# Cross-attention and coupled feed-forward: part of a first layer moved into attention slots, and the front of the feed-forward stage written in half dozens of products

## The chip, the cores and the metric

The kernel runs on one core of a Trainium2 chip. The metric is the device time of one execution in microseconds (us). Before the change it is 1096.31 us, the median of 3 runs (1096.15 to 1098.32).

## The reference

`x` is 64 batches of 256 tokens with 256 features, the context 64 batches of 120 keys with 256 features. All is float32.

```
n    = layernorm(x)
# attention, 16 heads of 16 features
s    = exp(log_C) * tanh(scale * (q_h . k_h) / 4)         # masked keys: -inf
x    = x + concat_h(softmax(s) @ v_h) @ W_out.T
# feed-forward: 3 cycles on u = layernorm(x)
gf   = sigmoid(gelu(gelu(mean_tokens(u) W1g + b) W2g + b) W3g + b)   # one number per batch
repeat 3 times:
    tf = sigmoid(gelu(gelu(gelu(u W1 + b1) W2 + b2) W3 + b3) W4 + b4)  # one number per token
    c  = 0.1 + range * (0.7 gf + 0.3 tf - 0.5) * 2
    u  = u + c * twist(u)            # twist permutes and negates quarters of the features
x    = x + u
```

The first layer is linear before its gelu, so the kernel holds `u W1` (in the tile `f_t`, "straight") and `twist(u) W1` (in `v_t`, "twisted") and updates these two with `c` instead of multiplying by W1 again in cycles 2 and 3.

## The kernel before, in words

**Stages.** The 64 batches are taken in 8 groups of 8. `slots()` yields one attention slot per batch, in software pipeline: in slot i TensorE makes the scores of batch i, the weighted values of batch i-1, the output projection of i-2, and transposes the normalised features of batch i-3 (`LAG` = 3). After the slot in which the last batch of a group has passed that transpose, `slots()` yields a feed-forward stage for the group. In the text, slot k (0 to 7) of a group is the slot with (i-3) mod 8 = k, so slot 7 is the last before the stage. Slots 0 to 7 of group 1 begin on TensorE at about 174, 182, 190, 199, 207, 215, 224 and 232 us of the span; its stage begins at 241 us.

**A slot.** Each engine has its own instruction stream, in an order that is written by hand; an instruction that waits for a semaphore holds all behind it on its engine.
- TensorE (from L1318): `scores(i,0)`, `weighted_values(i-1,0)`, `queries(i+1)`, `scores(i,1)`, `project(i-2,0)`, `keys(i+1)`, `weighted_values(i-1,1)`, `project(i-2,1)`, `norm_to_features(i-3)`. Both score products write PSUM banks 0 to 3, so `scores(i,1)` waits for the tanh of `scores(i,0)`. The weighted values write banks 4 and 5 (`PV_BANKS`), queries, keys and features bank 6, the projection bank 7.
- ScalarE (from L978): `tanh(i,0)`, `exp(i-1,1)`, `tanh(i,1)`, `exp(i,0)` (L880, L886; each 120x2048), `features(i-3)` (L896) from PSUM into `f_t`.
- VectorE (from L803): `attn_out(i-1,0)` (L678), `queries_out`, `stats` of a batch ahead, `combine` of a batch of the group before (L781, L782), `high_half`, `keys_out`, `attn_out(i-1,1)`, `divide`, `attn_features`, `residual`, `stats_2(i-2)` (L710, L716).
- GpSimd (from L552): `norm_2_scale` (needs `stats_2`), `query_scale` (needs `stats`), `norm_2` (L456, the input of `norm_to_features`), `twisted_part` (L511) and `x_part` (L520) of the group before, `query_hat` (L435, the input of `queries`), `low_half` (L529).

**The two halves.** The first layer's products run in float16, on a high and a low half of `f_t` and of the weights: three of the four combinations, two blocks of rows each, so 6 products of 128x128 by 128x512 for one half m of the output features. A group's features are taken in 4 chunks of 2 batches. `high_half` (VectorE, L725) rounds a chunk to float16, `low_half` (GpSimd, L529, once for each block k of rows) writes the rest. In the slots the chunks 0 and 1 are split: `HIGH_AT` = (2, 4) and `LOW_AT` = (3, 4, 5, 6) are the slots k of it. Chunks 2 and 3 are split in the stage: on GpSimd, the stage begins with `query_scale` and `query_hat` for two batches ahead, then `low_half` of chunk 2, the same for one more batch, then `low_half` of chunk 3.

**The stage.** Passes p = 0 to 11 are the 4 chunks in 3 cycles. TensorE runs `layer1_twisted` (L1179, banks 2 and 3), `layer1_straight` (L1192, banks 0 and 1), `layer2` (L1205), `layer3` (L1214), `layer4` (L1235, or L1232 from pass 3 on) and the global net; ScalarE the gelus (`gelu1` L912, `gelu2` L942, `gelu3` L954), `tanh4` (L966) and the copies out of PSUM (`twisted_out` L924, `straight_out` L934); VectorE `couple` (L734) and the updates of `f_t` and `v_t` (L747 to L772), which start with the tanh of pass 0. The stage's front is passes 0 to 3, in which the first layer is multiplied; there TensorE's order is

```
twisted(0) straight(0) global(0) | twisted(1) global(1) layer2(0) global(2) straight(1) layer3(0)
| twisted(2) layer4(0) layer2(1) straight(2) layer3(1) | twisted(3) layer4(1) layer2(2) straight(3) layer3(2)
| layer4(2) layer2(3) layer2(4) layer3(3)
```

with 12 products (both m) in each twisted and each straight.

Of the kernel before, what the change touches and what calls it, by code (L numbers as in the profile page):

```python
# [28 lines left out]
ALU = mybir.AluOpType  # L29
# [6 lines left out]
P = 128  # L36
# [8 lines left out]
def xattn_ffn_kernel(nc, x, ctx, mask, W_out, scale, log_C,  # L45
# [6 lines left out]
    EK = E // P  # L52
# [23 lines left out]
    with ExitStack() as stack:  # L76
# [108 lines left out]
        PV_BANKS = (4, 5)  # L185
# [44 lines left out]
        s_l1 = sem("s_l1")  # L230
        s_fhi, s_flo = sem("s_fhi"), sem("s_flo")
        s_uv = sem("s_uv")
        s_h1 = sem("s_h1")
# [17 lines left out]
        LOW_AT = (3, 4, 5, 6)  # L251
# [67 lines left out]
        def groups_before(i):  # L319

            return (i - LAG) // GROUP

# [261 lines left out]
        def _(eng):  # L584
# [88 lines left out]
            def attn_out(b, n):  # L673

                eng.wait_ge(s_pv, 2 * b + n + 1)
                if b >= 2:
                    eng.wait_ge(s_on, b - 1)
                eng.transpose(o_t[:, b % 2, 2 * n:2 * n + 2].rearrange("p c q r -> p (c q r)"),  # L678
                              banks(PV_BANKS[n])).then_inc(s_ot, 1)

# [38 lines left out]
            def high_half(g, chunk):  # L719
# [3 lines left out]
                if number >= 2:  # L723
                    eng.wait_ge(s_l1, 2 * EK * (number - 1))
                eng.tensor_copy(f_hl[:, number % 2, 0], f_t[:, :, chunk * CT:(chunk + 1) * CT]).then_inc(s_fhi, 1)  # L725

# [10 lines left out]
            def update_both(g, p):  # L737
# [5 lines left out]
                eng.wait_ge(s_uv, 2 * EK * (number + 1))  # L743
# [128 lines left out]
        def _(eng):  # L872
# [26 lines left out]
            def gelu1(g, p):  # L899
# [3 lines left out]
                for m in range(EK):  # L903
                    if cyc == 0:
                        eng.wait_ge(s_w, n_weights)
                        eng.wait_ge(s_vec0, N_SPLIT)
                        eng.wait_ge(s_l1, 2 * EK * (CHUNKS * g + chunk) + EK + m + 1)
# [7 lines left out]
            def twisted_out(g, chunk):  # L915

                number = CHUNKS * g + chunk
# [4 lines left out]
                for m in range(EK):  # L922
                    eng.wait_ge(s_l1, 2 * EK * number + m + 1)
                    eng.activation(v_t[:, m, tok], banks(V_BANKS[m]), ACT.Identity, scale=uv_scale[:, 0:1]) \  # L924
                       .then_inc(s_uv, 1)

            def straight_out(g, chunk):

                number = CHUNKS * g + chunk
                tok = slice(chunk * CT, (chunk + 1) * CT)  # L930
                eng.wait_ge(s_flo, EK * (number + 1))
                for m in range(EK):
                    eng.wait_ge(s_l1, 2 * EK * number + EK + m + 1)
                    eng.activation(f_t[:, m, tok], banks(U_BANKS[m]), ACT.Identity, scale=uv_scale[:, 0:1]) \  # L934
                       .then_inc(s_uv, 1)
# [40 lines left out]
            for kind, i in slots():  # L976
# [15 lines left out]
                else:  # L992
                    early = i * GROUP + GROUP + LAG
                    glob = banks(TR_BANK)[:, SMALL_AT:SMALL_AT + 3 * GROUP]
                    twisted_out(i, 0)
                    gelu1(i, 0)
                    straight_out(i, 0)
# [367 lines left out]
```

## Time and profile before

| what | us |
|---|---|
| median of 3 runs | 1096.31 |
| lowest, highest | 1096.15, 1098.32 |
| the profiled execution's own time | 1098.4 |
| its span, first to last instruction | 1096.6 |
| ScalarE busy in the span | 920.6 (84%) |
| TensorE busy (matmuls) | 979.9 (89%) |
| VectorE busy | 808.9 (74%) |
| GpSimd busy | 554.1 (51%) |

Times in the profile are microseconds from the start of the span. PE is TensorE, ACT ScalarE, DVE VectorE, POOL GpSimd. A timeline row reads: start, length, engine, line, operation, written tile<-read tiles, shapes, number of instructions merged into the row, and in brackets how long the engine had been idle and what released it. Matmuls overlap one another, so the next row often starts before the length of the last is over: the step from start to start is what a batch of matmuls costs.

### The profile page before, as it was taken

Reading aid. Unit: us, or ns where it says so; the run is one execution under the profiler, and the core shown is the slowest. Engines: PE = TensorE matmul, PEld = TensorE weight load, DVE = VectorE, ACT = ScalarE, POOL = GpSimd, SP = SyncE. Lnnn points to the kernel's source line nnn. Section 1 sums busy time; section 2 is a strip of 40 time slices with the busy share of each in tenths; the row PEclk is TensorE's granted clock in tenths of the full one; section 3 lists DMA queues with packets and bytes.
Section 4 is the critical chain, followed back from the end, with each engine's and each line's share of the span. In section 5 each row is a group of like instructions: output and inputs, shape, how many; then the busy total and the mean of one; then the engine's idle time right before and its main releaser. Section 6 shows DMA issues by size and latency. Waiting matters only on the chain.

```text
span 1096.6 us, 21849 instructions
## 1 busy us (share of the span) xinstructions
PE 979.9 (89%) x7260; PEld 530.3 (48%) x7260; DVE 808.9 (74%) x1738; ACT 920.6 (84%) x1153; POOL 554.1 (51%) x1053
## 2 busy tenths in 40 slices
PE   6899989899998999999999998989999899896993
PEld 4455435554355544554345543555435554453431
DVE  3888596985868666885869849698487867687285
ACT  3899778997799977998789977899779997795675
POOL 3367504884068810897028950488406881078104
PEclk7899999999999999999999999999999999998997
DMA  5433001430034200441005310143003420021002
GB/s 119 82 58 61 1 2 39 105 86 0 2 72 100 58 1 2 96 92 41 2 1 121 90 19 2 40 104 86 0 2 73 99 58 1 1 53 40 0 1 78
DMA packets 191119, 51.71 MB, mean 47 GB/s; under 512 B 165920, under 2 KB 174624, under 8 KB 191008
## 3 DMA queue, kind: packets, MB, share of 16 engines
q1 hardware_dynamic: 191008, 50.31, 21.6%
q8 instruction: 60, 0.98, 0.4%
q14 instruction: 51, 0.42, 0.1%
HBM read 33.37 MB, written 16.78 MB: 46 GB/s over the span
## 4 chain that ended last, share of the span: by engine, by line
ACT 41%; PE 30%; issue 13%; DVE 10%; SPq 2%; POOL 2%; DMA 1%; DVEq 0%; ACTq 0%; POOLq 0%
ACT probs L880 18%; ACT probs L886 14%; PE ps L1205 7%; PE ps L1192 6%; PE ps L1179 5%; ACT f_t L896 4%; PE ps L1116 3%; PE ps L1235 2%; DVE move_u L747 2%; DVE move_v L749 2%; PE ps L1214 2%; ACT h L912 2%; DVE f_t L753 2%; DVE coup L734 2%; PE ps L1147 1%
## 5 line engine op out<-in xcount | busy, mean ns | idle before, releaser
L880 ACT ACTIVATE probs<-ps,u_scale 120x2048 f32<-120x2048 f32 x128 | 257.6, 2012 | 21.4 <-PE ps L1116 21.4
L886 ACT ACTIVATE probs<-probs,exp_bias,clip 120x2048 f32<-120x2048 f32 x128 | 275.0, 2149 | 0.1
L1205 PE MATMUL ps<-h,w 128*128 128x512 f32 x384 | 184.4, 606 | 12.9 <-ACT h L912 12.1
L1116 PE MATMUL ps<-q_t,k_t 32*120 32x256 f32 x2048 | 150.0, 407 | 34.6 <-ACT probs L880 33.1
L475 POOL TENSOR_TENSOR c<-tok_c 128x16 f32<-128x16 f32 x8 | 1.8, 224 | 329.3 <-issue 329.3
L1147 PE MATMUL ps<-wo_t,of_t 128*128 128x256 f32 x512 | 144.5, 405 | 1.8 <-DVE xy L703 1.8
L678 DVE STREAM_TRANSPOSE o_t<-ps 128x512 f32<-128x512 f32 x128 | 90.8, 709 | 74.5 <-PE ps L1132 74.2
L1132 PE MATMUL ps<-probs,va 120*32 120x256 f32 x2048 | 138.4, 388 | 2.0 <-ACT probs L886 2.0
L1116 PEld LDWEIGHTS ps<-q_t,k_t 32*120 32x120 f32 x2048 | 95.1, 181 | 65.0 <-issue 60.5
L1147 PEld LDWEIGHTS ps<-wo_t,of_t 128*128 128x128 f32 x512 | 87.3, 190 | 51.0 <-issue 42.1
L1205 PEld LDWEIGHTS ps<-h,w 128*128 128x128 f32 x384 | 66.8, 188 | 87.7 <-issue 64.4
L942 ACT ACTIVATE h<-ps,b 128x512 f32<-128x512 f32 x96 | 65.6, 684 | 39.1 <-PE ps L1205 39.1
L912 ACT ACTIVATE h<-f_t,b 128x512 f32<-128x512 f32 x128 | 85.1, 715 | 11.6 <-DVE f_t L772 8.2
L1179 PE MATMUL ps<-f_hl,w1t_hl 128*128 128x512 f16 x384 | 90.1, 385 | 0.0
L734 DVE TENSOR_SCALAR coup<-coup,c_tok,c_batch 128x256 f32<-128x256 f32 x128 | 49.3, 427 | 54.7 <-ACT coup L966 53.6
L1192 PE MATMUL ps<-f_hl,w_hl 128*128 128x512 f16 x384 | 88.2, 379 | 0.0
L529 POOL TENSOR_TENSOR f_hl<-f_t,f_hl 128x512 f16<-128x512 f32 x64 | 75.2, 1186 | 19.9 <-DVE f_hl L725 19.9
L1132 PEld LDWEIGHTS ps<-probs,va 120*32 120x32 f32 x2048 | 53.8, 110 | 57.5 <-issue 19.5
L435 POOL TENSOR_SCALAR q_hat<-xy,neg,rstd 128x256 f32<-128x256 f32 x128 | 77.4, 613 | 4.2 <-POOL rstd L425 3.8
L456 POOL TENSOR_SCALAR f_hat<-xy,neg,rstd 128x256 f32<-128x256 f32 x128 | 74.4, 587 | 5.4 <-POOL rstd L446 5.4
L725 DVE CAST f_hl<-f_t 128x1024 f16<-128x1024 f32 x32 | 23.6, 738 | 70.0 <-PE ps L1192 70.0
L912 ACT ACTIVATE h<-ps,b,uv_scale 128x512 f32<-128x512 f32 x64 | 48.9, 776 | 31.2 <-PE ps L1192 31.1
(128 smaller groups left out, 1826.5 us busy)
## 6 DMA issues: line engine op xcount, KB each, us to landing
xy<-in_x_dram SPq DMA_DIRECT2D x64, 256.0 KB, 3.3
out_dram<-xy SPq DMA_DIRECT2D x64, 256.0 KB, 2.0
cbuf<-in_ctx_dram SPq DMA_DIRECT2D x64, 120.0 KB, 2.8
va<-in_ctx_dram SPq DMA_DIRECT2D x64, 120.0 KB, 3.6
tok_c<-coup SPq DMA_DIRECT2D x256, 0.5 KB, 2.0
move_v<-in_L_xattn_W_out_dram SPq DMA_DIRECT2D x1, 256.0 KB, 5.6
move_u<-in_L_ffn_cn_w_dram SPq DMA_DIRECT2D x1, 256.0 KB, 3.4
w<-in_L_ffn_cn_w_dram SPq DMA_DIRECT2D x1, 128.0 KB, 3.1
```

The lines of the kernel that those rows point to most:

```text
L435: eng.tensor_scalar(q_hat[:, at, t, :], xy[:, b % XR, t * E:(t + 1) * E], neg1[:, at, t:t + 1], rstd1[:, at, t:t + 1], ALU.add, ALU.mult). ...
L529: eng.tensor_tensor(f_hl[:, slot, 1, k], f_t[:, k, tok], f_hl[:, slot, 0, k], ALU.subtract) \
L678: eng.transpose(o_t[:, b % 2, 2 * n:2 * n + 2].rearrange("p c q r -> p (c q r)"), banks(PV_BANKS[n])).then_inc(s_ot, 1)
L880: eng.activation(probs[:, b % 2, n * HALF:(n + 1) * HALF, :].rearrange("k h q -> k (h q)"), banks(SCORE_BANK, 4)[0:KEYS, :], ACT.Tanh, sca ...
L886: eng.activation(p, p, ACT.Exp, scale=clip[0:KEYS, 0:1], bias=exp_bias[:, b:b + 1]).then_inc(s_exp, 1)
L912: eng.activation(h1[:, p % 2, m, :], source, ACT.Gelu, bias=b1[:, m:m + 1], scale=by) \
L1116: last = eng.matmul(banks(SCORE_BANK + r)[0:KEYS, odd * S:(odd + 1) * S], k_t[rows, b % 2, odd, n, :], q_t[rows, b % 2, n, :], start=True, ...
L1132: last = eng.matmul(banks(PV_BANKS[n])[j * SLOT:(j + 1) * SLOT, (c % 2) * S:(c % 2 + 1) * S], va[:, b % VR, h, :], probs[:, b % 2, h, :], ...
L1147: last = eng.matmul(banks(X_BANK)[:, t * E:(t + 1) * E], of_t[:, k, t * P:(t + 1) * P], wo_t[:, k, :], start=(k == 0), stop=(k == EK - 1))
L1179: last = eng.matmul(banks(V_BANKS[m]), w1t_hl[:, w, k, m * P:(m + 1) * P], halves[:, f, k, :], start=(n == 0), stop=(n == len(PRODUCTS) - 1))
L1192: last = eng.matmul(banks(U_BANKS[m]), w1_hl[:, w, k, m * P:(m + 1) * P], halves[:, f, k, :], start=(n == 0), stop=(n == len(PRODUCTS) - 1))
L1205: last = eng.matmul(banks(bank), w2[:, k, :], h1[:, p % 2, k, :], start=(k == 0), stop=(k == EK - 1))
```

## The change

For each group, the first layer of chunk 0 (four half dozens: twisted m = 0, 1, straight m = 0, 1) is computed in the slots 4 to 7, one half dozen a slot, into bank 5, and VectorE brings it to `v_t` or `f_t`. The weighted values use bank 4 alone. The stage then has only chunks 1 to 3 to multiply, and its order on TensorE and ScalarE is written out by half dozens. `low_half` is done in slots 2, 3, 5, 6.

```
-        PV_BANKS = (4, 5)
+        PV_BANK = 4
+        SIDE_BANK = 5
-        LOW_AT = (3, 4, 5, 6)
+        LOW_AT = (2, 3, 5, 6)
+        SIDE_AT = (4, 5, 6, 7)
+        SIDES = 2 * EK
...
             def high_half(g, chunk):                                    # VectorE
-                if number >= 2:
-                    eng.wait_ge(s_l1, 2 * EK * (number - 1))
+                if chunk == 2:
+                    eng.wait_ge(s_sl1, SIDES * (g + 1))
+                elif number >= 2:
+                    eng.wait_ge(s_ul1, EK * (...))
...
+            def side_out(g, part):                                      # VectorE
+                kind, m = part // EK, part % EK
+                eng.wait_ge(s_sl1, SIDES * g + part + 1)
...
+                dst = (v_t, f_t)[kind]
+                eng.tensor_scalar(dst[:, m, 0:CT], banks(SIDE_BANK), uv_scale[:, 0:1], None, ALU.mult).then_inc(s_side, 1)
...
                     if 0 <= nxt < NB:
                         keys_out(nxt)
+                    if side_of(i) is not None:
+                        side_out((i - LAG) // GROUP, side_of(i))
                     if 0 <= here < NB:
                         attn_out(here, 1)
...
             def weighted_values(b, n):                                  # TensorE
-                if after_ffn(b + 1):
-                    eng.wait_ge(s_h2, PASSES * groups_before(b + 1) - 1 + n)
-                elif b:
-                    eng.wait_ge(s_ot, 2 * (b - 1) + n + 1)
+                if after_ffn(b + 1) and n == 0:
+                    eng.wait_ge(s_h2, PASSES * groups_before(b + 1) - 1)
+                if 2 * b + n:
+                    eng.wait_ge(s_ot, 2 * b + n)
...
+            def layer1_side(g, part):                                   # TensorE
+                kind, m = part // EK, part % EK
+                halves = f_hl[:, CHUNKS * g % 2]
+                weights = (w1t_hl, w1_hl)[kind]
+                if part == 0:
+                    eng.wait_ge(s_vec0, N_SPLIT)
+                    eng.wait_ge(s_flo, EK * (CHUNKS * g + 1))
+                if part == 0 and g:
+                    eng.wait_ge(s_h2, PASSES * g)
+                elif part:
+                    eng.wait_ge(s_side, SIDES * g + part)
+                for n, (w, f, k) in enumerate(PRODUCTS):
+                    last = eng.matmul(banks(SIDE_BANK), weights[:, w, k, m * P:(m + 1) * P], halves[:, f, k, :],
+                                      start=(n == 0), stop=(n == len(PRODUCTS) - 1))
+                last.then_inc(s_sl1, 1)
...
                         if 0 <= nxt < NB:
                             queries(nxt)
+                        if side_of(i) is not None:
+                            layer1_side((i - LAG) // GROUP, side_of(i))
                         if 0 <= i < NB:
                             scores(i, 1)
```

`gelu1` of pass 0 now reads `f_t` (scale 1.0) after `s_side`, and `twisted_out`, `straight_out`, `layer1_twisted` and `layer1_straight` take one m at a time. The new front of the stage, with a half dozen written as t(chunk,m) or s(chunk,m), is

```
TensorE: global(0) t(1,0) t(1,1) s(1,0) s(1,1) global(1) layer2(0) global(2) t(2,0) layer3(0) t(2,1) layer4(0)
         layer2(1) s(2,0) layer3(1) s(2,1) layer4(1) t(3,0) layer2(2) t(3,1) layer3(2) s(3,0) layer4(2) s(3,1)
         layer2(3) layer2(4) layer3(3)
ScalarE: gelu1(0) global gelu, t_out(1,0) t_out(1,1) gelu1(1) global gelu, gelu2(0) global tanh, gelu3(0)
         s_out(1,0) s_out(1,1) tanh4(0) t_out(2,0) t_out(2,1) gelu2(1) gelu1(2,m0) gelu3(1) gelu1(2,m1) tanh4(1)
         s_out(2,0) s_out(2,1) t_out(3,0) gelu2(2) gelu3(2) t_out(3,1) gelu1(3,m0) tanh4(2) s_out(3,0) gelu1(3,m1)
         gelu1(4) gelu2(3) s_out(3,1) gelu3(3) gelu2(4) gelu1(5)
```

From pass 5 on nothing is changed.

## Rows read from the trace of the kernel before

**Rows 1.** The profile page: the chain that ended last, by engine.

```profile
ACT 41%; PE 30%; issue 13%; DVE 10%; SPq 2%; POOL 2%; DMA 1%; DVEq 0%; ACTq 0%; POOLq 0%
```

**Rows 2.** Busy time by stage: window, length, then each engine's busy us.

```profile
215.22:223.63 8.41, 7.56 (x83) 4.84 (x82) 7.47 (x19) 8.41 (x9) 6.57 (x13) 1.00 0.27 79
240.65:272.70 32.05, 30.98 (x138) 14.29 (x135) 18.26 (x41) 24.08 (x41) 14.93 (x25) 1.00 0.09 16
```

**Rows 3.** Timeline of ScalarE, slots 4 and 7 of group 1.

```profile
212.06 2.02 ACT L880 ACTIVATE probs<-ps,u_scale 120x2048 f32<-120x2048 f32 x1
...
237.31 2.00 ACT L880 ACTIVATE probs<-ps,u_scale 120x2048 f32<-120x2048 f32 x1
...
241.86 2.15 ACT L886 ACTIVATE probs<-probs,exp_bias,clip 120x2048 f32<-120x2048 f32 x1
```

**Rows 4.** Timeline of TensorE, slots 4 and 5 of group 1.

```profile
210.39 1.14 PE L1116 MATMUL ps<-q_t,k_t 32*120 32x256 f32 x16 [0.85 <-ACT probs L880]
...
215.22 1.14 PE L1116 MATMUL ps<-q_t,k_t 32*120 32x256 f32 x16
...
217.30 0.66 PE L1091 MATMUL ps<-ident,q_hat 128*128 128x128 f32 x4
218.80 1.14 PE L1116 MATMUL ps<-q_t,k_t 32*120 32x256 f32 x16 [0.85 <-ACT probs L880]
```

**Rows 5.** Timeline of GpSimd, slots 3 to 7 and stage of group 1.

```profile
203.53 0.32 POOL L422 TENSOR_SCALAR var<-mv 128x2 f32<-128x2 f32 x1 [0.59 <-DVE mv L658]
...
209.58 1.15 POOL L529 TENSOR_TENSOR f_hl<-f_t,f_hl 128x512 f16<-128x512 f32 x1
...
218.26 0.24 POOL L443 TENSOR_SCALAR var<-mv 128x2 f32<-128x2 f32 x1 [0.85 <-DVE mv L716]
...
225.31 1.09 POOL L435 TENSOR_SCALAR q_hat<-xy,neg,rstd 128x256 f32<-128x256 f32 x2
...
240.08 1.63 POOL L435 TENSOR_SCALAR q_hat<-xy,neg,rstd 128x256 f32<-128x256 f32 x2
...
250.00 2.27 POOL L529 TENSOR_TENSOR f_hl<-f_t,f_hl 128x512 f16<-128x512 f32 x2
```

**Rows 6.** Timeline of VectorE, slot 4 of group 1.

```profile
210.42 0.65 DVE L664 COPY q_t<-ps 128x512 f32<-128x512 f32 x1
...
213.87 0.72 DVE L678 STREAM_TRANSPOSE o_t<-ps 128x512 f32<-128x512 f32 x1 [0.37 <-PE ps L1132]
```

**Rows 7.** Timeline of TensorE, stage of group 1.

```profile
240.65 2.75 PE L1179 MATMUL ps<-f_hl,w1t_hl 128*128 128x512 f16 x12
...
254.43 0.65 PE L1214 MATMUL ps<-h,w 128*64 128x256 f32 x4
255.01 2.76 PE L1179 MATMUL ps<-f_hl,w1t_hl 128*128 128x512 f16 x12
257.62 1.03 PE L1235 MATMUL ps<-h,w4rep 128*128 128x256 f32 x4
```

**Rows 8.** Timeline of VectorE, stage of group 1: the couplings of passes 0 to 3.

```profile
259.40 1.12 DVE L734 TENSOR_SCALAR coup<-coup,c_tok,c_batch 128x256 f32<-128x256 f32 x2 [3.88 <-ACT coup L966]
...
267.85 0.73 DVE L734 TENSOR_SCALAR coup<-coup,c_tok,c_batch 128x256 f32<-128x256 f32 x2 [2.00 <-ACT coup L966]
...
274.61 0.73 DVE L734 TENSOR_SCALAR coup<-coup,c_tok,c_batch 128x256 f32<-128x256 f32 x2 [0.69 <-ACT coup L966]
...
280.80 0.73 DVE L734 TENSOR_SCALAR coup<-coup,c_tok,c_batch 128x256 f32<-128x256 f32 x2
```

**Rows 9.** Timelines of group 0: GpSimd in slot 3, TensorE in slot 4.

```profile
76.44 1.62 POOL L529 TENSOR_TENSOR f_hl<-f_t,f_hl 128x512 f16<-128x512 f32 x1
...
78.56 0.66 PE L1091 MATMUL ps<-ident,q_hat 128*128 128x128 f32 x4
```

**Rows 10.** Timeline of TensorE, stage of group 7, the last.

```profile
1015.18 4.62 PE L1179 MATMUL ps<-f_hl,w1t_hl 128*128 128x512 f16 x12
...
1033.64 1.03 PE L1235 MATMUL ps<-h,w4rep 128*128 128x256 f32 x4
```

More of the change, by code:

```diff
@@ L321, in groups_before, with uv_done, side_of @@
             return (i - LAG) // GROUP
+        def uv_done(g, chunk):
+            return 2 * EK * ((CHUNKS - 1) * g + chunk)
+        def side_of(i):
+            at = (i - LAG) % GROUP
+            return SIDE_AT.index(at) if i >= LAG and at in SIDE_AT else None
         def paired(p):
@@ L897, in features, with gelu1 @@
                                    ACT.Identity, scale=F_SCALE, accum_out=f_sum[:, k, at:at + 1]).then_inc(s_ft, 1)
-            def gelu1(g, p):
+            def gelu1(g, p, halves=range(EK)):
                 (cyc, chunk), n = slot_of(p), PASSES * g + p
@@ L902, in gelu1 @@
                     eng.wait_ge(s_l2, n - 1)
-                for m in range(EK):
-                    if cyc == 0:
+                for m in halves:
+                    if cyc == 0 and chunk == 0:
                         eng.wait_ge(s_w, n_weights)
-                        eng.wait_ge(s_vec0, N_SPLIT)
-                        eng.wait_ge(s_l1, 2 * EK * (CHUNKS * g + chunk) + EK + m + 1)
+                        eng.wait_ge(s_side, SIDES * (g + 1))
+                        source, by = f_t[:, m, 0:CT], 1.0
+                    elif cyc == 0:
+                        eng.wait_ge(s_ul1, EK * ((CHUNKS - 1) * g + chunk - 1) + m + 1)
                         source, by = banks(U_BANKS[m]), uv_scale[:, 0:1]
@@ L1169, in layer1_twisted @@
+            def layer1_twisted(g, chunk, m):
                 number = CHUNKS * g + chunk
                 halves = f_hl[:, number % 2]
-                eng.wait_ge(s_vec0, N_SPLIT)
                 eng.wait_ge(s_flo, EK * (number + 1))
-                for m in range(EK):
-                    if chunk == 0:
-                        eng.wait_ge(s_tanh, 2 * min(GROUP * g + GROUP + LAG, NB))
-                    else:
-                        eng.wait_ge(s_uv, 2 * EK * (number - 1) + m + 1)
-                    for n, (w, f, k) in enumerate(PRODUCTS):
-                        last = eng.matmul(banks(V_BANKS[m]), w1t_hl[:, w, k, m * P:(m + 1) * P], halves[:, f, k, :],
-                                          start=(n == 0), stop=(n == len(PRODUCTS) - 1))
-                    last.then_inc(s_l1, 1)
@@ L1183, in layer1_straight @@
-            def layer1_straight(g, chunk):
+                if chunk == 1:
+                    eng.wait_ge(s_tanh, 2 * min(GROUP * g + GROUP + LAG, NB))
+                else:
+                    eng.wait_ge(s_uv, uv_done(g, chunk - 2) + m + 1)
+                for n, (w, f, k) in enumerate(PRODUCTS):
+                    last = eng.matmul(banks(V_BANKS[m]), w1t_hl[:, w, k, m * P:(m + 1) * P], halves[:, f, k, :],
+                                      start=(n == 0), stop=(n == len(PRODUCTS) - 1))
@@ L1227, in layer4 @@
                 if paired(p):
[L1228 removed]
+                    eng.wait_ge(s_uv, uv_done(g, CHUNKS - 1))
                 for b in range(CB):
```

166 lines of the change are left out of this document (95 added, 71 removed).

## The prediction, made blind

> **What bounds the kernel now.** I read the chain that ended last first, then busy time by stage, then the timelines of one group, engine by engine. The chain [rows 1] is ScalarE's for 41% and TensorE's for 30%: no single engine holds the whole span. The stages tell why [rows 2]. An attention slot takes 8.41 us and ScalarE is busy for all 8.41 of them; TensorE is busy 7.56 of them. The front of the feed-forward stage takes 32.05 us and TensorE is busy 30.98 of them. So moving products from the front into the slots takes work from the stage where TensorE is full and gives it to one where it has some room. In a slot that room is 0.85 us, one gap, in which TensorE has finished the queries and waits for the tanh to free the score banks [rows 4].
>
> All below is worked out for group 1 on its own time axis; groups 2 to 6 repeat it. I call a time "shifted" when it is given less the delay that the slots have built up.
>
> **Slots, middle groups: what is added.** One half dozen on TensorE, at half of the 2.60 us from one dozen to what follows it (255.01 to 257.62) [rows 7]: 1.30 us. One evacuation on VectorE, PSUM to SBUF, 128x512: the copy of the same size takes 0.65 [rows 6]. `low_half` moves from slot 4 to slot 2 on GpSimd, 1.15. No DMA is moved or added; the weighted values lose a bank, but each waits only for the transpose of the product before, which VectorE starts right behind it (213.87, 0.72 long [rows 6]) and TensorE comes back 2.5 us later, so I cost that at nothing. If that transpose came late, it would hold TensorE; the side evacuation stands ahead of it on VectorE and delays it by some 0.15.
>
> *Step 1, the first half dozen waits.* It needs both low halves of chunk 0. The second is made in slot 3, last on GpSimd, before and after the change: 209.58 plus 1.15 [rows 5]. The low half added in slot 2 pushes it: 1.15, of which the 0.59 that GpSimd waited in slot 3 [rows 5] takes half. It ends at 211.28. TensorE has its queries done at 209.7 and would be ready, so the half dozen runs from 211.35 to 212.65 and `scores(i,1)` starts at 212.65 in place of 210.39 [rows 4]. Its tanh starts 1.18 later, at 213.83, in place of 212.06 [rows 3]: ScalarE loses 1.77 in slot 4.
>
> *Step 2, three slots at TensorE's pace.* Between `scores(i,1)` at 210.39 and the next slot at 215.22 TensorE has 4.83 of work without a gap [rows 4]; from there to the end of the queries 2.68 (217.30 less 215.22 plus 0.60); the half dozen 1.30. That is 8.81 a slot, over the 8.41 of ScalarE. Three of them bring `scores(i,1)` of slot 7 to 212.65 + 26.43 = 239.08.
>
> *Step 3, the queries come late.* `q_hat` on GpSimd hangs on `stats_2` and `stats`, which VectorE now ends later: its attention work in slot 4 begins at 216.3 instead of 213.87 [rows 6], as the weighted values do. GpSimd's slot 5 starts 2.4 later than at 218.26 [rows 5], `q_hat` ends at 228.8 instead of 226.4 [rows 5], TensorE wants it at 228.35. It waits 0.5 there and 0.2 in slot 7. Together 239.78; the tanh of slot 7 starts at 240.96 instead of 237.31 [rows 3]. **The slots cost 3.65 us a group.**
>
> **The stage, middle groups: what is taken away.** 24 products, 5.2 us of TensorE, and 4 copies of ScalarE. Shifted times from here, the last exponential at 241.86 [rows 3]. The stage now begins with the global net, which needs ScalarE's last features, so TensorE starts at 242.05, not 240.65 [rows 7]. The four half dozens of chunk 1 run until 247.6, then `layer2(0)` and the small nets until 250.1. (`gelu1(0)`, behind the exponential and its table load, ends at 246.5, in time.)
>
> *Step 4, a second wait for GpSimd.* t(2,0) needs the low halves of chunk 2, which end at 250.00 + 2.27 = 252.27 [rows 5]. Before, TensorE came for them at 255.01 [rows 7] and they cost nothing; now it comes at 250.1. GpSimd stands behind `stats` of VectorE, whose slot 7 ends 0.43 later (shifted). So t(2,0) starts at 252.75 and 2.6 us of the 5.2 are given back. `layer3(0)`, which needs nothing of this, is queued behind it.
>
> *Step 5, to the couplings.* t(2,0) 1.30, `layer3(0)` 0.58 (254.43 to 255.01 [rows 7]), t(2,1) 1.30: `layer4(0)` at 255.93 against 257.62 [rows 7]. The coupling of pass 0 starts at 257.7 against 259.40 [rows 8]. VectorE needs 6.07 us a pass (267.85 to 274.61, less 0.69) and waited 2.00 and 0.69 before passes 1 and 2 [rows 8]. With TensorE without a gap from 252.75 on, `layer4(1)` is at 262.5, `layer4(2)` at 269.6, so pass 1 does not wait (264.1) and pass 2 hardly (270.5). Pass 3 has its tanh at 277.3, behind `gelu1(4)` and `gelu1(5)` on ScalarE, and its coupling at 278.0 against 280.80 [rows 8]. From there VectorE is without a gap in both. **The stage gives 2.8 less 0.05, 2.75 us.**
>
> Net of a middle group: 3.65 - 2.75 = +0.9, six times: +5.4.
>
> **Group 0.** No group before it, so GpSimd is idle when its low halves come: the one of slot 3 ends at 78.06, TensorE's queries at 79.2 [rows 9]. Step 1 falls away. TensorE's excess of 0.4 a slot for four slots, less the lead that the scores had, is 1.2; the stage gives 2.4. Net -1.2.
>
> **Group 7.** From its slot 5 on there are no new scores: the half dozens run in empty time, and no batch ahead keeps GpSimd from chunk 2. The stage starts slow (12 products in 4.62 us [rows 10] against 2.75 [rows 7]); with that, 24 products, `layer2(0)`, t(2,0), `layer3(0)` and t(2,1) put `layer4(0)` at 1029.0 against 1033.64 [rows 10]. Another 1.1 comes from the waits of VectorE as in step 5. Net -5.7.
>
> **Sum:** 5.4 - 1.2 - 5.7 = -1.5 us. The profiled execution has a span of 1096.6 and a time of 1098.4; the sum gives 1095.1 and 1096.9. The median before is 1096.31, 2.1 under the profiled one; against it 1094.8, and I say 1095.
>
> **Bounds of what the trace does not show.** The side evacuation: nothing if it falls in VectorE's wait (0.37 before the transpose [rows 6]), 0.65 in each of four slots if VectorE's round were the bound; I take 0.15, since VectorE is busy 7.47 of 8.41. The switch between float16 and float32 products: within the 1.30, or 0.1 more each way by the dozen's own length of 2.75 against 2.60 [rows 7]. The stage's written-out order: at worst only the 1.7 of pass 0 is kept (a loss of 1.05 a group), at best pass 3's coupling comes as early as VectorE can, 276.6 (a gain of 1.4). For six groups that is from -8 to +6.
>
> **A row and a rule.** The same two-instruction `q_hat` took 1.09 in slot 5 and 1.63 in slot 7 [rows 5], so something of VectorE holds GpSimd now and then for some 0.5. The Trainium skill (SBUF - State Buffer, Who interferes with whom) says that VectorE and GpSimd share a port pair as a lock, that the loser waits for the whole instruction, and that a VectorE instruction with one input from PSUM outside the 2-port modes does not take it. By that rule the side evacuation adds nothing to GpSimd, as in my sum, but VectorE's two-input instructions, which move against GpSimd's, may; no row here shows the new alignment.
>
> **Rivals.**
> A. *The first wait does not bite* (step 1): chunk 0's low halves are there in time. Then `scores(i,1)` of slot 4 starts at 210.8, the slots cost 1.8, a middle group nets -0.95: -5.7 - 6.9 = -12.6, 1084. Against it: the row at 209.58 stands in every group from 1 on.
> B. *Neither wait bites*: the whole 5.2 of TensorE pays, the stage gives 5.4 and the slots cost 1.2; -4.2 in seven groups and -5.7: -35, 1061. Against it stand the two rows of L529 [rows 5]. For it, only that GpSimd is idle much of the span.
> C. *Slower: GpSimd becomes the bound of slots 4 to 7.* Its chain of scale, features, twisted, x and query parts is held by VectorE once more in each of the slots 3, 5 and 6, 0.43 to 0.54 each (1.63 less 1.09 [rows 5]). All three lie on TensorE's path to the first half dozen or to the queries: +1.3 a middle group, +7.8, so 1103. It decides from the point where the hold is more than 0.3 a group, as then the six groups eat what groups 0 and 7 give.
>
> **Chances.** My forecast 0.45, A 0.20, B 0.07, C 0.28. 0.2% of this kernel is 2.2 us, about what a measurement can tell from no change. My own case lies 1.5 under and moves by 6 either way: of its 0.45, 0.18 is faster, 0.15 the same, 0.12 slower. A and B are faster; C is slower but for 0.02. So faster 0.45, same 0.17, slower 0.38. My case's own range is 1087 to 1101; the range takes in A and C with their spread, 1082 to 1107, and leaves B out.
>
> **What would show it.** In the profile after: GpSimd's `low_half` in slot 3 ends at 211.3 on group 1's axis and TensorE's first half dozen starts right behind it, released by it; the tanh of `scores(i,1)` in slot 4 shows an idle of 1.8; slots 5 to 7 take 8.8 to 9.3; at the stage's front TensorE idles 2 to 3 us ahead of t(2,0), released by L529, and VectorE's wait before pass 1's coupling is gone. In group 7 neither wait is seen, and its stage's couplings start 4.6 earlier after the last features. I am wrong if a middle group gets more than 2 us shorter, or if the idle time sits with VectorE's evacuation or the single bank of the weighted values.

## The result, and the profile after

The kernel after the change takes **1117.68 us** (median of 4 runs, 1116.52 to 1119.74) against 1096.63 us for the kernel before: ratio 1.019, 95% interval 1.0172 to 1.0207. It is slower, by 21 us; the forecast was 1095.0 and the range ended at 1107. The profiled execution took 1119.74 us with a span of 1118.0, which is 21.3 over the profiled execution before (1098.4); its eight groups, cut as in the table below, add up to 21.5 more.

To read where it went I cut each group at four points of the timelines: the start of ScalarE's last `tok_th` of the group before, the end of the group's last exponential, VectorE's coupling of pass 0, its coupling of pass 3, and the group's own `tok_th`.

| us | slots | last exponential to coupling 0 | coupling 0 to 3 | coupling 3 to `tok_th` | group |
|---|---|---|---|---|---|
| before, group 1 | 66.29 | 15.39 | 21.39 | 26.91 | 129.99 |
| after, group 1 | 70.28 | 15.78 | 20.83 | 26.91 | 133.81 |
| after, group 2 | 70.29 | 17.08 | 20.83 | 26.91 | 135.11 |
| before, group 0 | 113.68 | 15.39 | 21.39 | 27.26 | 177.72 |
| after, group 0 | 114.75 | 15.92 | 20.83 | 26.90 | 178.40 |
| before, group 7 | 41.06 | 35.58 | 21.39 | 25.00 | 123.04 |
| after, group 7 | 41.06 | 32.25 | 20.83 | 24.99 | 119.14 |

Groups 3, 4 and 6 are as group 1 (133.8 to 134.1), group 5 as group 2 (135.08). A middle group got 3.2 to 5.1 longer where +0.9 was forecast, group 0 0.7 longer where -1.2 was, and group 7 3.9 shorter where -5.7 was. The slots were forecast nearly right (3.65); the second column was not (-1.7 forecast, +0.4 to +1.7 measured). Group 1 of the kernel after starts 0.69 later on the axis than before, so a time of its slots compares with one of before less 0.69; in its stage, 4.67 are to be taken off (the last exponential ends at 248.68 against 244.01 [rows 3]).

The page, first the engines, then the chain that ended last by engine (it answers to [rows 1]), then three of the costliest groups (busy time, mean ns | idle time before them):

```profile
PE 994.2 (89%) x7260; PEld 529.0 (47%) x7260; DVE 829.7 (74%) x1770; ACT 905.6 (81%) x1121; POOL 554.5 (50%) x1053
...
PE 46%; DVE 15%; POOL 14%; issue 11%; ACT 11%; SPq 2%; DMA 0%; DVEq 0%; POOLq 0%; ACTq 0%
...
L912 ACT ACTIVATE probs<-ps,u_scale 120x2048 f32<-120x2048 f32 x128 | 252.9, 1976 | 39.8 <-PE ps L1156 39.0
...
L1234 PE MATMUL ps<-f_hl,w1t_hl 128*128 128x512 f16 x288 | 80.6, 427 | 20.5 <-POOL f_hl L543 20.5
```

GpSimd went from 2% to 14% of the chain though its busy time did not change; ScalarE from 41% to 11%. Both waits for GpSimd stand in the groups: the tanh now waits 39.0 us for scores (21.4 before), and `layer1_twisted` 20.5 us for the low halves (seven times 2.9), which before it did not wait for at all.

The slots of group 1. GpSimd's timeline answers to [rows 5]:

```profile
211.07 1.16 POOL L543 TENSOR_TENSOR f_hl<-f_t,f_hl 128x512 f16<-128x512 f32 x1
...
228.74 1.09 POOL L449 TENSOR_SCALAR q_hat<-xy,neg,rstd 128x256 f32<-128x256 f32 x2
...
250.17 1.11 POOL L439 TENSOR_TENSOR rstd<-var,minus_half 128x2 f32<-128x2 f32 x1
...
252.63 0.77 POOL L436 TENSOR_SCALAR var<-mv 128x2 f32<-128x2 f32 x1
...
255.61 2.27 POOL L543 TENSOR_TENSOR f_hl<-f_t,f_hl 128x512 f16<-128x512 f32 x2
```

TensorE's timeline of slots 4 to 7 answers to [rows 4]:

```profile
210.08 0.66 PE L1131 MATMUL ps<-ident,q_hat 128*128 128x128 f32 x4
212.34 1.46 PE L1220 MATMUL ps<-f_hl,w1t_hl 128*128 128x512 f16 x6 [1.60 <-issue]
213.72 1.14 PE L1156 MATMUL ps<-q_t,k_t 32*120 32x256 f32 x16
...
220.63 0.66 PE L1131 MATMUL ps<-ident,q_hat 128*128 128x128 f32 x4
221.12 1.46 PE L1220 MATMUL ps<-f_hl,w1t_hl 128*128 128x512 f16 x6
222.51 1.14 PE L1156 MATMUL ps<-q_t,k_t 32*120 32x256 f32 x16
...
229.88 0.65 PE L1131 MATMUL ps<-ident,q_hat 128*128 128x128 f32 x4 [0.40 <-POOL q_hat L449]
...
238.94 0.66 PE L1131 MATMUL ps<-ident,q_hat 128*128 128x128 f32 x4 [0.20 <-POOL q_hat L449]
...
240.82 1.14 PE L1156 MATMUL ps<-q_t,k_t 32*120 32x256 f32 x16
```

and ScalarE's answers to [rows 3]:

```profile
214.93 1.97 ACT L912 ACTIVATE probs<-ps,u_scale 120x2048 f32<-120x2048 f32 x1 [1.76 <-PE ps L1156]
...
242.03 1.97 ACT L912 ACTIVATE probs<-ps,u_scale 120x2048 f32<-120x2048 f32 x1 [0.27 <-PE ps L1156]
```

TensorE has its queries done at 210.7 and stands until the low half ends at 212.23; the profile names no releaser ("issue"), but the half dozen starts 0.11 behind that end. The tanh waits 1.76. This is step 1 as it was worked out.

The front of the stage, TensorE, answers to [rows 7]:

```profile
254.62 0.39 PE L1315 MATMUL ps<-gh,g3rep 64*128 64x8 f32 x2
257.93 2.74 PE L1234 MATMUL ps<-f_hl,w1t_hl 128*128 128x512 f16 x6 [2.92 <-POOL f_hl L543]
260.61 0.84 PE L1269 MATMUL ps<-h,w 128*64 128x256 f32 x4
261.38 1.47 PE L1234 MATMUL ps<-f_hl,w1t_hl 128*128 128x512 f16 x6
262.68 1.03 PE L1290 MATMUL ps<-h,w4rep 128*128 128x256 f32 x4
```

Here is what was not forecast. The wait is there, 2.92 long and released by GpSimd, but the six products behind it take 2.68 to the start of the next row, where the same six take 1.30 a row further down. The windows of this stretch (length, then busy us of PE, PEld, DVE, ACT, POOL, then the granted clock of TensorE as a mean over the window) show the clock fall:

```profile
254.00:256.00 2.00, 1.01 (x4) 0.29 (x2) 0.39 (x1) 0.97 (x3) 1.83 (x4) 1.00 0.02 4
256.00:258.00 2.00, 0.07 (x1) 0.07 (x2) 0.79 (x1) 0.00 (x0) 1.91 (x3) 0.90 0.00 0
258.00:260.00 2.00, 2.00 (x5) 0.67 (x6) 0.00 (x0) 0.00 (x0) 1.75 (x5) 0.50 0.00 0
260.00:262.00 2.00, 2.00 (x9) 0.60 (x8) 0.00 (x0) 0.50 (x2) 2.00 (x3) 0.74 0.00 0
```

While TensorE stood idle its granted clock fell from 1.00 to 0.50, from 2.4 to 1.2 GHz, and it came back only while `layer3(0)` ran. That the fall follows from the idle time, and that it is what makes the products slow, is tested by e4 below. In groups 2 and 5 the clock came back later still: the second half dozen was slow too (group 2, TensorE's timeline).

```profile
391.75 2.74 PE L1234 MATMUL ps<-f_hl,w1t_hl 128*128 128x512 f16 x6 [2.93 <-POOL f_hl L543]
394.42 1.12 PE L1269 MATMUL ps<-h,w 128*64 128x256 f32 x4
395.47 2.48 PE L1234 MATMUL ps<-f_hl,w1t_hl 128*128 128x512 f16 x6
```

VectorE's timeline beside GpSimd's two stretched rows of the stage (L439 and L436 above) holds its copies of chunks 2 and 3 to float16:

```profile
250.56 0.68 DVE L741 CAST f_hl<-f_t 128x1024 f16<-128x1024 f32 x1
...
252.67 0.69 DVE L741 CAST f_hl<-f_t 128x1024 f16<-128x1024 f32 x1 [0.56 <-PE ps L1246]
```

VectorE's couplings of passes 0 to 3 in group 1 answer to [rows 8]: pass 0 is 0.4 later than before once 4.67 are taken off, pass 1 waits no more, and the waits moved on to passes 2 and 3.

```profile
264.47 0.99 DVE L761 TENSOR_SCALAR coup<-coup,c_tok,c_batch 128x256 f32<-128x256 f32 x2 [7.68 <-ACT coup L994]
...
270.70 0.73 DVE L761 TENSOR_SCALAR coup<-coup,c_tok,c_batch 128x256 f32<-128x256 f32 x2
...
277.48 0.73 DVE L761 TENSOR_SCALAR coup<-coup,c_tok,c_batch 128x256 f32<-128x256 f32 x2 [0.72 <-ACT coup L994]
...
285.30 0.74 DVE L761 TENSOR_SCALAR coup<-coup,c_tok,c_batch 128x256 f32<-128x256 f32 x2 [1.76 <-ACT coup L994]
```

### The profile page after: what moved, and what is told of

Same layout as the page of the kernel before. It is cut to its first block, busy times and chain, and to the rows that moved or that the text cites. A ratio compares the mean times of both kernels' runs of the same rounds, so it can differ in the third digit from the quotient of the medians.

```text
span 1118.0 us, 21903 instructions
## 1 busy us (share of the span) xinstructions
PE 994.2 (89%) x7260; PEld 529.0 (47%) x7260; DVE 829.7 (74%) x1770; ACT 905.6 (81%) x1121; POOL 554.5 (50%) x1053
## 4 chain that ended last, share of the span: by engine, by line
PE 46%; DVE 15%; POOL 14%; issue 11%; ACT 11%; SPq 2%; DMA 0%; DVEq 0%; POOLq 0%; ACTq 0%
PE ps L1260 8%; PE ps L1156 7%; PE ps L1187 5%; PE ps L1234 5%; PE ps L1246 4%; PE ps L1172 4%; ACT probs L912 4%; PE ps L1269 3%; PE ps L1220 3%; ACT probs L918 3%; POOL q_hat L449 2%; POOL rstd L439 2%; POOL f_hl L543 2%; ACT h L946 2%; DVE move_u L798 2%
## 5 line engine op out<-in xcount | busy, mean ns | idle before, releaser
L912 ACT ACTIVATE probs<-ps,u_scale 120x2048 f32<-120x2048 f32 x128 | 252.9, 1976 | 39.8 <-PE ps L1156 39.0
L918 ACT ACTIVATE probs<-probs,exp_bias,clip 120x2048 f32<-120x2048 f32 x128 | 268.6, 2099 | 0.1
L1260 PE MATMUL ps<-h,w 128*128 128x512 f32 x384 | 186.5, 608 | 12.7 <-ACT h L946 11.4
L761 DVE TENSOR_SCALAR coup<-coup,c_tok,c_batch 128x256 f32<-128x256 f32 x128 | 47.4, 412 | 82.1 <-ACT coup L994 82.1
L946 ACT ACTIVATE h<-f_t,b 128x512 f32<-128x512 f32 x144 | 95.7, 714 | 12.5 <-DVE f_t L802 9.0
L1234 PE MATMUL ps<-f_hl,w1t_hl 128*128 128x512 f16 x288 | 80.6, 427 | 20.5 <-POOL f_hl L543 20.5
L982 ACT ACTIVATE h<-ps,b 128x256 f32<-128x256 f32 x96 | 45.1, 470 | 62.3 <-PE ps L1269 62.2
L683 DVE TENSOR_TENSOR k_t<-ps,parity 128x480 f32<-128x480 f32 x64 | 42.0, 656 | 49.1 <-PE ps L1140 49.1
L449 POOL TENSOR_SCALAR q_hat<-xy,neg,rstd 128x256 f32<-128x256 f32 x128 | 71.6, 569 | 4.2 <-POOL rstd L439 3.8
L525 POOL TENSOR_SCALAR twisted<-xy,neg,b_r 128x256 f32<-128x256 f32 x112 | 70.7, 641 | 1.2 <-POOL x_add L489 1.1
```

Source lines behind the costliest of these rows:

```text
L449: eng.tensor_scalar(q_hat[:, at, t, :], xy[:, b % XR, t * E:(t + 1) * E], neg1[:, at, t:t + 1], rstd1[:, at, t:t + 1], ALU.add, ALU.mult). ...
L912: eng.activation(probs[:, b % 2, n * HALF:(n + 1) * HALF, :].rearrange("k h q -> k (h q)"), banks(SCORE_BANK, 4)[0:KEYS, :], ACT.Tanh, sca ...
L918: eng.activation(p, p, ACT.Exp, scale=clip[0:KEYS, 0:1], bias=exp_bias[:, b:b + 1]).then_inc(s_exp, 1)
L946: eng.activation(h1[:, p % 2, m, :], source, ACT.Gelu, bias=b1[:, m:m + 1], scale=by) \
L1234: last = eng.matmul(banks(V_BANKS[m]), w1t_hl[:, w, k, m * P:(m + 1) * P], halves[:, f, k, :], start=(n == 0), stop=(n == len(PRODUCTS) - 1))
L1260: last = eng.matmul(banks(bank), w2[:, k, :], h1[:, p % 2, k, :], start=(k == 0), stop=(k == EK - 1))
```

## The experiments

Theory after the result: two waits on GpSimd's in-order stream cost the time, and the second costs more than its length, since TensorE's clock falls in it. Rivals: TensorE's pace in the slots is the cost and the first wait only covers it; the single bank or the side evacuation; the stage's new order itself. Each kernel differs from the kernel after by the edit shown, unless it says "from the kernel before". The runs were made in three batches, each with the kernel before beside them: its median was 1096.6 for e1 to e8 and 1097.8 for e9 to e11. Each ratio is to the kernel before of the same batch; a difference between two of these kernels from different batches carries that 1.2 us.

### The wait ahead of t(2,0): e2, e7, e4

**e2_low_first** takes chunk 2's halves ahead of the batches ahead, on both engines:

```
 VectorE, stage:  + high_half(i, 2)  then stats of the batches ahead   (was: two of them, high_half, the rest)
 GpSimd, stage:   + low_half(i, 2, k) then query_scale, query_hat      (was: two of them, low_half, the rest)
```

> The changed kernel with chunk 2 split first in the stage, on VectorE and on GpSimd, ahead of the statistics and query parts of the batches ahead. Theory (the second wait for GpSimd and the clock that falls in it cost the stage): TensorE no longer idles 2.9 us before t(2,0), the granted clock stays at 1.00, t(2,0) takes 1.3 instead of 2.7; seven groups gain 4.3 each (groups 2 and 5 some 1.3 more), 1117.7 - 33 = about 1085 us, faster than the kernel before. Rival (the written-out order of the front, or ScalarE, is the next bound at once): less than half of it, 1101 us or more.

Measured: **1085.26** (4 runs, 1085.05 to 1085.29), ratio to the kernel before 0.9893 (0.9878 to 0.9908). Confirmed to 0.3 us: 32.4 us less than the kernel after. TensorE's timeline of the same stretch of group 1:

```profile
249.58 0.39 PE L1310 MATMUL ps<-gh,g3rep 64*128 64x8 f32 x2
249.90 1.47 PE L1229 MATMUL ps<-f_hl,w1t_hl 128*128 128x512 f16 x6
251.29 0.65 PE L1264 MATMUL ps<-h,w 128*64 128x256 f32 x4
```

No idle time, no slow product. From the last exponential to coupling 0 it is 11.33 in every group from 0 to 6, against 15.39 before and 15.75 to 17.08 after.

**e7_before_low_first** is the same edit, made to the kernel before.

> The kernel before with chunk 2 split first in the stage, as in e2_low_first. Theory (before the change TensorE came for these halves 2.7 us after they were ready, so their order was free): 1096.6 us, within 1.5. Rival (the earlier split helps by itself, so e2_low_first's gain is not the removal of a wait that the change made): 3 us faster or more.

Measured: 1096.81 (10 runs), ratio 1.0003 (0.9993 to 1.0012). Confirmed. The order of GpSimd's work cost nothing until TensorE came for it 5 us earlier: e2's gain belongs to the wait that the change opened.

**e4_filler** leaves the wait as it is, and fills it with work that no one uses:

```
                     global_net(i, 2)
+                    if i < NGROUPS - 1:
+                        for _ in range(11):      # constants, into the side bank, which is empty here
+                            eng.matmul(banks(SIDE_BANK), w1_hl[...], w1t_hl[...], start=True, stop=True)
                     layer1_twisted(i, 2, 0)
```

> The changed kernel with 11 products of constants into the free bank 5 just before t(2,0), in groups 0 to 6: TensorE is busy while it waits, nothing else is moved. Theory (the clock falls because TensorE idles there): granted clock 1.00 through the wait, t(2,0) takes 1.3 instead of 2.7 and the start of t(2,0) stays where it was; 1.4 us a group in seven groups and 1.3 more in groups 2 and 5, 12 us in all: about 1105.5 us. Rival (the slow half dozens have another cause, such as their own operands or the switch of precision): t(2,0) stays at 2.7 and the time at 1117 us or more.

Measured: **1106.28** (1105.41 to 1106.34), ratio 1.0082 (1.0066 to 1.0099). Confirmed: 77 products more, and 11.4 us faster than without them. TensorE's timeline:

```profile
253.43 2.55 PE L1369 MATMUL ps<-w1t_hl,w_hl 128*128 128x512 f16 x11
256.42 1.47 PE L1234 MATMUL ps<-f_hl,w1t_hl 128*128 128x512 f16 x6 [0.44 <-POOL f_hl L543]
257.82 0.65 PE L1269 MATMUL ps<-h,w 128*64 128x256 f32 x4
```

and a window of it, with the clock at 1.00 where it was 0.50:

```profile
256.00:258.00 2.00, 1.58 (x8) 0.69 (x10) 0.00 (x0) 0.00 (x0) 1.66 (x5) 1.00 0.00 0
```

The stretch to coupling 0 is 14.32 in each of the groups 0 to 6. Nothing else was touched, so it splits the loss of the stretch against e2: the idle time itself costs 14.32 - 11.33 = 3.0 a group, the clock 1.4 to 1.6 in five groups and 2.75 in groups 2 and 5.

### The waits in the slots: e1, e3, e8, e6

**e1_side_late** moves the first half dozen, of slot 4 only, behind `project(old, 1)`, where its low half is long made, and its evacuation behind `stats_2`.

```
-                        if side_of(i) is not None:
+                        if side_of(i):                       # parts 1 to 3 stay ahead of scores(i,1)
                             layer1_side(...)
...
                         project(old, 1)
+                    if side_of(i) == 0:
+                        layer1_side((i - LAG) // GROUP, 0)
```

> The changed kernel with the first half dozen of each group (and its evacuation) moved to the end of slot 4, where chunk 0's low halves are ready. Theory (the first wait for GpSimd costs the slots): the tanh of the second scores of slot 4 no longer waits (1.76 us there before); TensorE still has 8.8 us of work a slot, so of the 4.0 us that the slots of a middle group grew by, about 1.3 go and 2.7 stay. Time 1117.7 - 8 = about 1109.5 us. Rival (the wait is only hidden time of another one: TensorE's pace or late query parts take over in full): less than 2 us gained, 1116 us or more.

Measured: 1114.30 (1112.84 to 1115.85), ratio 1.0158 (1.0141 to 1.0176). A miss: 3.4 us of the 8 expected. The tanh of slot 4 waits no more, but other waits took its place (ScalarE, slots 4 and 7):

```profile
216.11 0.38 ACT L930 ACTIVATE f_t<-ps 128x256 f32<-128x256 f32 x1 [0.56 <-PE ps L1202]
...
239.53 1.97 ACT L914 ACTIVATE probs<-ps,u_scale 120x2048 f32<-120x2048 f32 x1 [0.77 <-PE ps L1158]
```

TensorE has the half dozen more to do in slot 4 wherever it stands, so a part of the 1.76 only covered that, and `q_hat` is 0.69 late in slot 7. The slots took 69.23 in place of 70.28. Group 7 gave 2.8 back: it took 121.94 in place of 119.14. So the rival was half right: by itself, the first wait is worth 1.0 a group, not 1.77. The time is a rough measure of it: the profiled executions differ by 6.9, not 3.4, because in this one groups 0, 2 and 5 also pay less in the stage (14.05, 15.82 and 15.83 to coupling 0 against 15.92, 17.08 and 17.07), mainly because fewer of their products are slow.

**e3_both** is e1 and e2 together.

> Both edits together. Theory (two separate waits, in different stages): the gains add, 8 + 33 = 41 us, about 1077 us. Rival (one feeds the other, so that they overlap): no better than the better one of the two by more than 2 us.

Measured: 1083.79 (1082.64 to 1084.28), ratio 0.9878 (0.9864 to 0.9893). A miss, as it must be after e1: 1.5 better than e2, 8 expected. The slots gain their 1.0 in five groups and 0.6 in group 4; groups 0 and 7 lose 1.5 and 3.1.

**e8_pool_order** keeps the half dozens where the change put them and turns GpSimd's order in each slot, on top of e2:

```
                 norm_2(...)
+                low_half(...)            # those that TensorE waits for
+                query_hat(new)
                 twisted_part, x_part     # of the group before: no one waits for them soon
-                query_hat(new)
-                low_half(...)
```

> The kernel e2_low_first with GpSimd's low half and query part ahead of the twisted and x parts of the group before, in every attention slot. Theory (the first wait and the late queries both come from GpSimd's order): TensorE no longer waits for the low halves of chunk 0 in slot 4 nor for the queries in slots 6 and 7; only its pace of 8.8 us is left, and the slots of a middle group cost about 1.8 more than before instead of 4.0: 68.1 us, the time about 1072 us. Rival (as when the first half dozen was moved to the slot's end, TensorE's pace takes the time over): the slots gain 1 us a group or less, 1079 us or more. Slower than 1085: the twisted and x parts, now last, hold up VectorE's combine.

Measured: **1070.26** (1069.18 to 1070.71), ratio 0.9754 (0.9738 to 0.9771). Confirmed, and the best kernel of the study: 26.3 us faster than the kernel before, 47.4 faster than the one after. The slots take 67.62, 1.33 more than before; one slot of group 1 in the busy windows (it answers to [rows 2], first row):

```profile
216.00:224.80 8.80, 8.80 (x96) 5.35 (x92) 8.30 (x21) 8.64 (x9) 7.71 (x15) 1.00 0.40 90
```

TensorE is busy for all 8.80 of it: step 2's 8.81. The profile marks a wait of ScalarE in slots 5, 6 and 7, one and the same 0.16, and none elsewhere in these slots; the rest of the 0.39 that a slot is longer lies in steps too short for it to mark:

```profile
221.64 1.97 ACT L907 ACTIVATE probs<-ps,u_scale 120x2048 f32<-120x2048 f32 x1 [0.16 <-PE ps L1151]
```

So of the 3.99 that the slots of the kernel after cost, 2.6 (70.22 - 67.62) are GpSimd's order. The 1.33 that stays I put down to TensorE's pace, as it has no gap in these slots; that is read from the trace, and no run took work from TensorE on top of e8.

**e6_four** is e2 with four of the six products in each half dozen of the slots.

> The kernel e2_low_first with 4 of the 6 products in each half dozen of the slots; left out are those with the low half of the weights, so the first layer of chunk 0 is less exact. Theory (TensorE's pace of 8.8 us in slots 4 to 7 is the largest part of what they cost): 0.43 less a slot puts it at 8.4, ScalarE's own pace; the slots of a middle group fall from 70.2 to about 68.2 us, the time from 1085.3 to about 1073 us. Rival (the waits for GpSimd and for VectorE's evacuation set the slots, not TensorE's work): less than 0.5 us a group, 1082 us or more.

Measured: 1078.24 (1076.82 to 1078.68), ratio 0.9828 (0.9813 to 0.9843). 7.0 us of the 12 expected: 1.2 a group, not 2.0. With less on TensorE, ScalarE still waits 1.32 for the first scores of slot 4 and 0.41 in slot 6; TensorE, with less to do, stands 1.59 before the half dozen of slot 4 and 0.82 before the queries of slot 6, the latter released by `q_hat`: GpSimd sets these. A third off the products gives less than half of what e8's turned order gives for nothing.

### The order of the stage: e9, e10, e11

**e9_old_front** is e2 with the front written as before, in dozens, for chunks 1 to 3 (twisted(1) | global(1) layer2(0) global(2) straight(1) layer3(0) | twisted(2) layer4(0) layer2(1) straight(2) ...), on TensorE and ScalarE.

> The kernel e2_low_first with the front of the stage in the order of before (whole dozens, the loop over passes) for chunks 1 to 3; the slots as they are. Theory (what the moved products give, TensorE's work, does not hang on the half dozens; the rewrite is worth its 0.56 us between the couplings of passes 0 and 3, plus the earlier third-layer product): 0.5 to 2 us a group slower than e2_low_first, 1089 to 1101 us. Rival (the rewrite is worth nothing): 1085.3, within 1.5.

Measured: 1101.17 (1100.34 to 1102.68), ratio 1.0041 (1.0026 to 1.0056). Just past the slow end of what was expected. The rewritten front is worth 15.9 us by the medians (15.3 by the profiled executions), 2.1 a group. 1.63 of it lies before coupling 0: twisted(1) alone does not bridge the time to the global net's gelu, so TensorE stands once more, and then does straight(1) ahead of t(2,·):

```profile
247.60 0.28 PE L1296 MATMUL ps<-gh,g 128*64 128x8 f32 x2 [1.56 <-ACT gh L1020]
...
250.04 2.76 PE L1229 MATMUL ps<-f_hl,w_hl 128*128 128x512 f16 x12
```

This idle time of 1.56 left the clock where it was, at 1.00:

```profile
246.00:248.00 2.00, 0.44 (x4) 0.38 (x4) 1.79 (x9) 1.99 (x5) 1.91 (x3) 1.00 0.00 0
```

Without the rewrite, moving chunk 0 into the slots loses against the kernel before even with e2's order of the stage. With e8's order of the slots added it might win; that kernel was not run.

**e10_order_alone** is the kernel after with e8's order of GpSimd in the slots, and its own stage, wait included.

> The changed kernel with GpSimd's low half and query part first in each attention slot, as in e8_pool_order, but with the stage as it was changed, so that t(2,0) still waits. Theory (slots and stage are separate terms): the slots of a middle group take 67.6 us as in e8_pool_order, 2.6 less than in the changed kernel, the stage is as in the changed kernel (15.8 to 17.1 us to the first coupling); 6 x 2.6 = 16 less, about 1102 us. Rival (with the slots shorter, the stage's wait for GpSimd grows by as much): 1112 us or more.

Measured: 1098.55 (1094.11 to 1100.37, 10 runs), ratio 1.0004 (0.9989 to 1.0018). The slots came as expected, 67.64; the time was 3.5 us lower than expected, as the stage lost less in some groups. TensorE's timeline of its groups 1 and 5:

```profile
254.09 1.61 PE L1234 MATMUL ps<-f_hl,w1t_hl 128*128 128x512 f16 x6 [2.93 <-POOL f_hl L543]
255.63 1.12 PE L1269 MATMUL ps<-h,w 128*64 128x256 f32 x4
256.69 2.45 PE L1234 MATMUL ps<-f_hl,w1t_hl 128*128 128x512 f16 x6
...
779.34 1.47 PE L1234 MATMUL ps<-f_hl,w1t_hl 128*128 128x512 f16 x6 [2.93 <-POOL f_hl L543]
780.74 0.65 PE L1269 MATMUL ps<-h,w 128*64 128x256 f32 x4
781.33 1.47 PE L1234 MATMUL ps<-f_hl,w1t_hl 128*128 128x512 f16 x6
```

and the window of group 5 in which its idle time ends, with the clock at 1.00:

```profile
778.00:780.00 2.00, 0.66 (x4) 0.31 (x4) 0.20 (x1) 0.00 (x0) 1.83 (x5) 1.00 0.00 0
```

The same idle time of 2.93, and behind it slow products in group 1 and none in group 5: the stretch to coupling 0 is 15.92 and 14.33, so 1.6 apart (14.33 again in group 6). 14.33 is e4's figure, where the clock never fell.

**e11_before_order** makes the same turn of GpSimd's slots in the kernel before.

> The kernel before with GpSimd's low half and query part first in each attention slot. Theory (there ScalarE sets the slots' pace and nothing of GpSimd is on the path): 1096.6 us, within 1.5. Rival (GpSimd's order held that kernel too): 3 us faster or more.

Measured: 1097.71 (10 runs), ratio 1.0005 (0.9996 to 1.0014): nothing, as expected. Like e7 it shows that the order was free until something waited for it.

### The single bank: e5

**e5_one_bank**, from the kernel before: both weighted values into bank 4, with the change's waits.

> The kernel before with one PSUM bank for the weighted values, as the change has it, and nothing else. Theory (the bank costs nothing: VectorE's transpose comes 1.1 us behind each product and TensorE returns after 2.5): 1096.6 us, within 1.5. Rival (part of the slots' 4.0 us a group is this wait): 3 us slower or more, at least 0.5 us a group.

Measured: 1097.29 (10 runs), ratio 1.0003 (0.9994 to 1.0012), and in the middle groups the slots and the stage up to coupling 3 take what they took before, to 0.03. The bank given up costs nothing. The side evacuation was not taken out in any run; e8 has it, with TensorE busy for the whole slot, so nothing shows that it costs.

## Why the prediction was wrong, step by step

- **Step 1, the first wait: right.** Low half at 212.23 on an axis that runs 0.69 late, so 211.54 where 211.28 stood; tanh idle 1.76 where 1.77 stood. The tanh itself starts at 214.24 shifted by the 0.69, 0.4 later than the 213.83 worked out: the low half ends 0.3 later and the half dozen takes 1.38 where 1.30 stood. ScalarE's exponential before it ends 0.4 later as well, so the idle time came out right all the same. That 0.4 is what the slots missed by.
- **Step 2, TensorE's pace of 8.81: right.** From `scores(i,1)` of slot 4 to that of slot 5 it took 8.79, and 8.80 in e8. The sum owes some luck: the half dozen takes 1.39 to the next row where 1.30 stood, and the queries 0.49 where 0.60 stood, two errors of 0.1 that cancel. What e1 adds is that steps 1 and 2 are not two prices to be had back one by one: take the wait away and 1.0 comes back, take GpSimd's order away and 2.6 does.
- **Step 3, the queries late: right.** 0.40 and 0.20 against 0.5 and 0.2. The slots cost 3.99 against 3.65.
- **Step 4, the second wait: the step that failed, by its price.** The mechanism is as written: TensorE comes at 250.3 (shifted; 250.1 forecast), idles 2.92 (2.6 forecast), is released by `low_half`. The forecast priced that wait at its length and gave the products behind it the 1.30 and 0.58 of a TensorE that had not stood still. They took 2.68 and 0.77. With the wait ending 0.5 later than worked out (253.26 shifted, not 252.75), that is 0.5 + 1.4 + 0.2 = 2.1, and it puts `layer4(0)` at 258.0 shifted in place of 255.93. Two groups paid 1.3 more. e4 shows the clock to be the cause. A number for slow products was in the forecast's own rows, used for group 7 alone: there 12 products take 4.62 where they take 2.75 elsewhere [rows 10, 7]. TensorE had been idle there for 1.83, 0.99 and 4.84 us within the 13 us before, though, so that row gave a price for a fallen clock and did not say whether one idle time of 2.6 us would bring the fall on. Of the 2.9 by which group 1 missed (+3.8 against +0.9), 2.1 are this step, 0.3 the slots and 0.5 the second term of step 5.
- The 0.5 on GpSimd: two of its small instructions ahead of the low halves (L439 and L436 above) took 1.11 and 0.77, each while a copy of VectorE to float16 ran (L741, 250.56 to 251.24 and 252.67 to 253.36). The same two took 0.71 and 0.23 in the kernel before, where one `q_hat` took 0.43 more instead; 0.94 less 0.43 is the 0.5. The Trainium skill (SBUF - State Buffer, Who interferes with whom) says that the loser of the shared port pair waits for the whole instruction of the other; the lengths fit that, no run here took the VectorE instructions away. This is rival C's mechanism, at 0.5 of its 1.3 us a group, in the stage and not in the slots.
- **Step 5, the couplings: wrong, for the most part because of step 4.** Coupling 0 came at 259.8 shifted, not 257.7. The second term, that passes 2 and 3 would hardly wait, was too good as well, and by itself: even in e2, with no wait before t(2,0), coupling 0 to 3 is 20.83, a gain of 0.56 where 1.1 was forecast. In the kernel after VectorE waits 0.72 and 1.76 before passes 2 and 3. What spaces the couplings is TensorE: it is busy for 20.18 of these 20.83 us in the kernel after and in e2 alike.
- **Group 0:** the slots +1.07 as forecast (1.2); its GpSimd has batches ahead in the stage just as the others, and it paid the same second wait. **Group 7:** no wait, as forecast; to coupling 0 it won 3.3 where 4.6 was forecast. The slow start remains (12 products in 4.04, at 1043.45). The last product that makes features stands 0.8 further behind the last exponential than before (15.26 against 14.44), and from there to `layer4(0)` it takes 15.20 against 19.36; no run took this apart.
- **Rivals.** A and B fell with the two waits. C gave the right sign, but its place, the slots, was not where the forecast missed: that is the stage. The range left out the case that happened since no case had a price for a slow TensorE in the middle groups. The chance of slower, 0.38, was too low for the same reason.

What each edit is worth, from the runs: moving chunk 0 costs 1.33 a middle group in the slots, with TensorE busy throughout. It gives 4.06 before coupling 0 and 0.56 after it, if the rewritten front is there (2.1 of it) and if GpSimd's two orders are turned. As it was made, GpSimd's order ate 2.6 in the slots and 4.4 to 5.8 in the stage of each group.

## What to carry to other kernels

When work is moved to an earlier place, look up for every input when it is made, by which engine and behind what in that engine's order; an order that cost nothing before costs nothing only as long as nobody comes earlier, and turning it was worth 47 us here. Price an idle time of TensorE of some 3 us as its length plus a range for the products behind it, from nothing to all of them at half the clock, and take the price of a slow product from a place in the same trace where TensorE starts after a pause. And when a wait is taken away, ask what it covered: e1 got back 1.0 of 1.77, e8, which turned the order behind both waits, 2.6.

## What the hardware showed that was not expected

- An idle time of 2.9 us in a stage in which TensorE is otherwise busy was enough to bring its granted clock from 1.00 to 0.50. The six products behind it took up to 2.68 in place of 1.30, and it was up to two half dozens until the clock was back. Shorter idle times in that stage left it at 1.00: 1.56 in e9, and 1.03 ahead of the global net in the kernel after. That is no promise for other places: in group 7 of the kernel before it was down (0.50 from 1006 on) soon after an idle time of 1.83 (1002.6 to 1004.4).
- The price of one and the same idle time differs from stage to stage: 0 (e10, groups 5 and 6), 1.4 to 1.6, or 2.75 us (groups 2 and 5 of the kernel after). It may well make a kernel's runs uneven too, though only one execution of each has a trace: 1094.11 to 1100.37 over 10 runs of e10, against 1085.05 to 1085.29 over 4 of e2, which has no such idle time. The Trainium skill (TensorE: Matmul & The Clock Gate, Part 1) says that a throttled array is the default state which activity releases, and that the count of slow products varies from run to run because the window looked at runs free. The rows agree with both: the clock came back while TensorE worked, and one and the same idle time of 2.93 cost slow products in some stages and none in others.
- Eleven useless products in each of seven groups made the kernel 11.4 us faster (e4).
